# Transposing a feed-forward activation tile with one DMA instead of identity products and PSUM copies

## What is computed

```python
def _bitlinear(x, w, b):
    xn = _layer_norm(x)
    xq = _activation_quant(xn)      # round(x * 127 / max|x|), clipped, / scale
    wq = _weight_quant(w)           # -1, 0, 1 times a scale
    return jnp.einsum('bsd,fd->bsf', xq, wq) + b
h = _bitlinear(x, w1, b1)           # 512 -> 2048
h = jax.nn.gelu(h, approximate=False)
return _bitlinear(h, w2, b2)        # 2048 -> 512
```

## Time and profile before

| | |
|---|---|
| median of 3 runs | 1193.89 us |
| lowest and highest run | 1190.55 and 1193.91 us |
| span of the profiled execution | 1187.8 us |
| its own time | no other than the span is shown; the median of the runs is 6.1 us more |
| mean granted TensorE clock | 0.944 |
| TensorE busy in the span | 1066.7 us, 90% |
| VectorE, ScalarE, GpSimd | 894.3 us, 721.0 us, 610.7 us |
| stage of the change | 237 to 405 us |

### The profile page before, as it was taken

How to read it: one execution, slowest core, us unless ns; L and a number is a source line. 1 busy time by engine, 2 the same in 40 slices (tenths; PEclk the granted TensorE clock), 3 DMA queues, 4 the chain that set the end, 5 groups by cost and what they waited for, 6 DMA issues and landing times. The chain is left out here.

```text
span 1187.8 us, 25724 instructions
## 1 busy us (share of the span) xinstructions
PE 1066.7 (90%) x9595; PEld 800.0 (67%) x9691; DVE 894.3 (75%) x1650; ACT 721.0 (61%) x1134; POOL 610.7 (51%) x629
## 2 busy tenths in 40 slices
PE   5999997679999899968999998788999799999995
PEld 4777776635554567727777776488776688888883
DVE  5589998978888798667888888578985556555538
ACT  4565772669899555638888877376454345545430
POOL 4444445635555322337788888421586355555520
PEclk9999998979999999979999999856999899999998
DMA  8573531043334212331222220096597567778877
GB/s 306 185 252 123 165 91 63 1 151 107 106 107 140 108 32 95 93 110 28 55 57 58 58 56 19 2 347 226 153 263 243 178 227 242 245 242 279 310 280 293
DMA packets 75744, 181.10 MB, mean 152 GB/s; under 512 B 9920, under 2 KB 12118, under 8 KB 74700
## 3 DMA queue, kind: packets, MB, share of 16 engines
q1 hardware_dynamic: 59292, 135.90, 34.4%
q0 software_dynamic: 8544, 24.68, 6.6%
q10 hardware_dynamic: 7792, 18.96, 5.2%
HBM read 128.49 MB, written 44.47 MB: 146 GB/s over the span
## 5 line engine op out<-in xcount | busy, mean ns | idle before, releaser
L470 PE MATMUL ps_y<-kv,toep 128*128 128x288 f32 x640 | 157.8, 409 | 3.6 <-PEq L173 2.0
L470 PEld LDWEIGHTS ps_y<-kv,toep 128*128 128x128 f32 x640 | 122.1, 192 | 38.7 <-DMA toep<-taps_padded 2.6
L1662 POOL TENSOR_TENSOR vw<-at_pf,kw 128x1024 bf16<-128x1024 f32 x64 | 136.6, 2134 | 2.7 <-ACT kw L1722 2.7
L164 POOL TENSOR_TENSOR kv<-kx 128x1024 f32<-128x1024 f32 x32 | 60.6, 1894 | 85.4 <-PE ps_y L470 35.8
L2648 POOL DMA_INDIRECT expert_results<-e_yo,target x47 | 70.3, 1496 | 55.3 <-ACT e_yo L2695 55.3
L1718 ACT ACTIVATE at_pf<-ps_st 128x1024 f32<-128x1024 f32 x64 | 65.5, 1024 | 40.7 <-PE ps_st L1858 36.5
L1769 DVE TENSOR_REDUCE at_negmax<-ps_s 128x4 f32<-128x1024 f32 x64 | 78.3, 1224 | 2.8 <-PE ps_s L1819 0.9
L1138 PEld LDWEIGHTS ps_eg<-e_xT,e_w 128*128 128x128 bf16 x1128 | 67.9, 99 | 14.9 <-issue 2.2
L1138 PE MATMUL ps_eg<-e_xT,e_w 128*128 128x128 bf16 x1128 | 71.9, 221 | 3.9 <-DVE e_xT L2756 3.9
L1077 PE MATMUL ps_fH<-w1T,f_qaT 128*128 128x512 bf16 x253 | 64.6, 400 | 9.8 <-PEq L643 5.5
L2749 DVE COPY e_w<-expert_weights 128x4096 bf16 x47 | 57.7, 1227 | 19.6 <-issue 19.6
(11 more groups left out here) (470 smaller groups left out, 3163.0 us busy)
## 6 DMA issues: line engine op xcount, KB each, us to landing
e_parts<-down_parts SPq DMA_DIRECT2D x47, 512.0 KB, 4.5
w_raw<-in_L_ffn_w ACTq DMA_DIRECT2D x32, 512.0 KB, 4.5
toep<-taps_padded SPq DMA_DIRECT2D x32, 256.0 KB, 3.6
f_draw<-in_L_ffn_rw SPq DMA_DIRECT2D x16, 512.0 KB, 4.3
down_parts<-f_dparts SPq DMA_DIRECT2D x16, 512.0 KB, 2.9
expert_weights<-expert_results SPq DMA_DIRECT2D x16, 512.0 KB, 9.9
x_res<-in_x SPq DMA_DIRECT2D x4, 1024.0 KB, 11.1
c_in<-in_ctx SPq DMA_DIRECT2D x4, 1024.0 KB, 14.2
```

The source lines that it names most:

```text
L164: pool.tensor_tensor(pairs[:, :, :, 0:HD0], x[:, :, 0:HD0].unsqueeze(2).broadcast_to([P, ROWS_N, WIDE, HD0]), sliding_rows(x, 0, 1, WIDE), ...
L470: last = pe.matmul(y[:, l * B:(l + 1) * B, :, WIDE - 1:], toep[h % 2][:, (DC - 1 - l + m) * P:(DC - l + m) * P], kv[h % 2][:, m * B:(m + 1 ...
L1662: pool.tensor_tensor(pl[u % 4][:, :, :, :], pf[u % 2][:, :, :, :], ph[u % 4][:, :, :, :], ALU.subtract)\
```

## The change

TensorE's 16 identity products for `f_qb`, the PSUM tiles' copies on ScalarE and VectorE and their semaphore `qbT_psum` are gone. In their place SP issues one `dma_start_transpose` a tile, from `f_qb` in SBUF (128 x 2048 bf16, 512 KB) to `f_qbT` in SBUF (128 x 16 x 128), ahead of the store and the load of the same turn. It waits for the rounding of the tile, and from tile 2 on for the down product of the tile two before it, which read the same `f_qbT` buffer. Its semaphore rises by 16 for a transfer, one semaphore for each buffer. `down(t)` waits once for the whole transfer, and `round_h(t)` from tile 2 on waits until the transfer of tile t-2 has read `f_qb`. The PSUM tiles `ps_fQ` stay, for the bias rows that are turned in the first steps.

```diff
--- before.py
+++ after.py
@@ -792,7 +792,7 @@
         qa_ready, qaT_psum, qaT_ready = quantised.qa_ready, quantised.qaT_psum, quantised.qaT_ready
         h_psum, gelu_done, dequant_kept = sem("hp"), sem("gelu"), sem("dk")
         rstd_ready, centred, quant_ready, h_scaled, qb_ready = (sem(n) for n in ("rstd", "cent", "quant", "hsc", "qb"))
-        qbT_psum, y_psum, y_added, biased = (sem(n) for n in ("qbTp", "yp", "ya", "biased"))
+        y_psum, y_added, biased = (sem(n) for n in ("yp", "ya", "biased"))
         parts_ready, parts_psum, rows_ready = quantised.parts_ready, quantised.parts_psum, quantised.rows_ready
         qbT_ready = [sem("qbT0"), sem("qbT1")]
         d_loaded, d_stored = ([sem(f"{n}{i}") for i in range(2)] for n in ("dl", "ds"))
@@ -807,6 +807,8 @@
         others_var, others_rstd = sem("ov"), sem("ors")
         GROUPS = (FIRST_TILES, OTHER_TILES)
 
+        DMA_INC = 16
+        turns_up_to = lambda t, p: (t - p) * (DMA_INC // 2) + DMA_INC
         runs = lambda j: not known(j) or 0 <= j < NT
         later = lambda j: not known(j) or j >= 2
 
@@ -842,10 +844,17 @@
                         row = ROWS[place] + 2 * e
                         sp.dma_start(rows[row:row + 2, :], k.ins[name][e, :].rearrange("(c p) -> c p", p=P)).then_inc(ahead_loaded, 16)
 
+            def turn_qb(t):
+                sp.wait_ge(qb_ready, t + 1)
+                if t >= 2:
+                    sp.wait_ge(y_psum, t - 1)
+                sp.dma_start_transpose(qbT[t % 2][:, :, :], qb[t % 2][:, :]).then_inc(qbT_ready[t % 2], DMA_INC)
+
             load(0)
             load(1)
             load_ahead()
             for e in range(E_N):
+                turn_qb(e)
                 sp.wait_ge(d_low, e + 1)
                 sp.dma_start(expert_down_parts(k)[e, :, :], d_parts[e % 2][:, :, :].rearrange("p h n -> p (h n)")).then_inc(d_stored[e % 2], 16)
                 if e + 2 < E_N:
@@ -874,10 +883,6 @@
                 scales.normalised(link, dve, OTHER_TILES)
                 scales.quantisers(k, link, dve, OTHER_TILES)
 
-            def copy_qbT(t, p):
-                dve.wait_ge(qbT_psum, t * 2 + 2)
-                dve.tensor_copy(qbT[p][:, 8:, :], psQ[1][:, :, :]).then_inc(qbT_ready[1], 1)
-
             def centre(t, p):
                 dve.wait_ge(gelu_done, t * 2 + 2)
                 link(dve.tensor_scalar(col(p, NEG_MEAN), col(p, SUM), col(p, OTHER_SUM), -1.0 / FF, ALU.add, ALU.mult))
@@ -898,6 +903,8 @@
 
             def round_h(t, p):
                 dve.wait_ge(h_scaled, t + 1)
+                if later(t):
+                    dve.wait_ge(qbT_ready[p], turns_up_to(t, p) - DMA_INC)
                 dve.tensor_scalar(qb[p][:, :], h[p][:, :], ROUND, None, ALU.subtract).then_inc(qb_ready, 1)
 
             def add_y(t, p):
@@ -944,8 +951,6 @@
                     round_h(n, p)
                 if runs(n + 1):
                     farthest(n + 1, 1 - p)
-                if runs(n):
-                    copy_qbT(n, p)
                 if runs(n + 1):
                     scale_of(n + 1, 1 - p)
 
@@ -983,10 +988,6 @@
                 act.wait_ge(squared, t + 1)
                 act.activation(col(p, VAR), col(p, SQUARE_SUM), ACT.Identity, scale=1.0 / FF, bias=k.small[:, 3:4]).then_inc(var_ready, 1)
 
-            def copy_qbT(t, p):
-                act.wait_ge(qbT_psum, t * 2 + 1)
-                act.activation(qbT[p][:, 0:8, :], psQ[0][:, :, :], ACT.Copy).then_inc(qbT_ready[0], 1)
-
             def scale(t, p):
 
                 act.wait_ge(quant_ready, t + 1)
@@ -1085,21 +1084,11 @@
                                          b1_parts[0:BIAS_ROWS, f * 512:(f + 1) * 512], start=False, stop=True)
                     last.then_inc(h_psum, 1)
 
-            def transpose_qb(t, p):
-                pe.wait_ge(qb_ready, t + 1)
-                for g in range(2):
-                    if not known(t) or t:
-                        pe.wait_ge(qbT_ready[g], t)
-                    for c in range(8):
-                        last = pe.transpose(psQ[g][:, c, :], qb[p][:, (8 * g + c) * P:(8 * g + c + 1) * P], k.ident_b[:, :])
-                    last.then_inc(qbT_psum, 1)
-
             def down(t, p):
                 if not known(t) or t:
                     pe.wait_ge(y_added, t)
+                pe.wait_ge(qbT_ready[p], turns_up_to(t, p))
                 for c in range(FC):
-                    if c % 8 == 0:
-                        pe.wait_ge(qbT_ready[c // 8], t + 1)
                     last = pe.matmul(psY[:, :], qbT[p][:, c, :], k.w2T[:, c * D:(c + 1) * D],
                                      start=(c == 0), stop=(c == FC - 1))
                 last.then_inc(y_psum, 1)
@@ -1109,8 +1098,6 @@
                     up(n + 1, 1 - p)
                 if runs(n + 2) and not (known(n) and n == -2):
                     transpose_qa(n + 2, p)
-                if runs(n - 1):
-                    transpose_qb(n - 1, 1 - p)
                 if runs(n - 2):
                     down(n - 2, p)
 
```

## The result

Kernel after: median of 7 runs 1188.61 us (1186.04 to 1190.20); kernel before, on the same chip: median of 7 runs 1193.79 us. **The ratio is 0.995, with a 95% interval of 0.993 to 0.9971: 5.2 us faster, by the interval 3.5 to 8.4 us.** In a second comparison, after 12 runs against before 35, the ratio is 0.9955 (0.9933 to 0.9976) and the medians are 3.7 us apart.

The account below looks back on a forecast made before the run. The prediction took the 9.04 us cycle of VectorE and GpSimd to bound the loop, not TensorE. Head -2.3 and tail -0.4 us gave 1193.9 - 2.7 = 1191.2 us, range 1186 to 1205.

Parts of the forecast that it names:

- rival D: In the looped tiles TensorE is the bound after all: eleven periods fall by 1.06 us, time 1179; chance 0.08.
- the ring: In the feed-forward loop VectorE and GpSimd wait for each other every tile; this 9.04 us cycle sets the period.
- part 2: PSUM copies removed: VectorE's 16 x 0.68 = 11 us become longer waits; ScalarE's removal counts only at the head and the tail.
- the head: At tile 0 ScalarE is freed of its copy and wait; tile 1's rounding starts 2.3 us earlier, bounds 0 and 2.7.
- the transfer: SP's 512 KB transposing transfer lands 4.6 us after the rounding, between 2.9 and 6.4; it costs the loop nothing.
- rival A: Transfers on one queue set the period: at 16 us each near 1295 us, at 10 us +11 us; chance 0.20.
- the split case: Eight SBUF-to-SBUF transfers of 64 KB, issued within 4.94 us, last landing at 6.4 us: upper estimate for the transfer.
- the tail: Last down product waits for the landing, runs 1.5 us slow, ends 404.4 against 404.51: gain 0.1 us, called 0.4.
- the sum: Gains at the head and the tail together: -2.3 - 0.4 = -2.7 us, bounds -5.0 and -0.6.
- Rival B: Landing in 6.4 to 9 us: the loop holds, the tail pays; at 9 us +2 us, 1196; chance 0.09.
- the last step of the working: Whole kernel: median 6.1 us above the 1187.8 us span, untouched by the change, so 1193.9 - 2.7 = 1191.2 us.
- no difference: Whole kernel's time within about 0.3%, 3.6 us, of before; chance 0.50, against 0.28 faster and 0.22 slower.

Follow-up runs that it names:

- experiment 1: Kernel after with 16 identity products of a constant put back on TensorE each tile, nobody waiting for them: 1189.68 us, ratio 0.9961 to the kernel before.
- experiment 4: Kernel after with the transposing transfer issued later, behind the store of the expert parts: 1196.49 us, ratio 1.0017 to the kernel before.
- 2: Kernel after with GpSimd's inverse root for the next tile moved ahead of its expert-weight split: 1190.74 us, ratio 0.9962 to the kernel before.
- 3: Kernel before with GpSimd's inverse root for the next tile moved ahead of its expert-weight split: 1196.89 us, ratio 1.0023 to the kernel before.
- 9 to 12: Inverse root between GpSimd's cast and subtraction: kernel after 1176.04 us; after with products back 1179.92; kernel before 1188.77; after with tile 15 by products 1178.40.
- Experiment 8: Kernel before with both PSUM copies on VectorE, TensorE's products kept, no transposing transfer: 1188.98 us, ratio 0.9985 to the kernel before.
- The second execution of after: Kernel after, unchanged, measured and profiled once more: 1186.08 us, ratio 0.9955 to the kernel before, stage 164.32 us.
- the second pair of traces: Both kernels unchanged, profiled once more: before 1192.54 us, stage 168.80 us; after 1186.08 us, stage 164.32 us.

## Why the prediction was right, and where not

**Right, the bound.** "Nothing of TensorE, nor any DMA, is in it": the 9.04 us period stayed to 0.01 us when TensorE's products went, stayed when they came back (experiment 1), stayed when the transfer landed 4.5 us later (experiment 4), and moved only when the order of GpSimd's work did (2, 3 and 9 to 12). TensorE's 82.30 of 84 us was occupancy, not a bound (rival D). Still, it had little to spare: "were the ring shorter by a microsecond, TensorE would be the bound and the removal would count" held, and sooner than that. With the products TensorE needs 8.9 us a tile, so 0.3 us off the 9.2 were enough. Two things were missing from the sentence. Without the products it is VectorE, at 8.65 us, and not TensorE that is full next. And the 0.68 us copy that part 2 wrote off as a longer wait then counts as well: the kernel before is at 8.90 us in the loop, where the kernel after with the products but without the copy stays at 8.65 up to tile 9. That is less than 0.68 in part because the collision is lighter there (L616 1.31 and L617 0.43 us in every other tile).

**Right, the head.** Forecast 2.3 us with tile 1's rounding at 266.06; measured 2.43 us, at 265.60 with a stage that began 0.36 us earlier. Experiment 8 has ScalarE's part of the cause at work without the transfer. The bound of 2.7 us held.

**Right, the transfer.** Forecast 4.6 us, measured 4.3 us median, 4.4 us for the last one; rival A (10 to 16 us each) is out. The nearest rows, one issue of 512 KB, led to it; the split case of eight 64 KB transfers would have led to 6.4. Of the two figures of the Trainium skill, "DMA: Bandwidth & Descriptors" (2.0 us by its 261 GB/s) was low by half as an estimate, and "VectorE: DVE Perf Modes" (an estimate of 21 us, from 1309 ns a block) five times high. The measurement decides: whatever a single block takes, sixteen in one transfer take 4.3 us. The queue was priced less well: I gave SP's issue no length of its own, and it is 1.3 to 2.0 us in place of 0.34 for a plain store, 3.33 when it comes right behind one.

**Right, the mechanism of the tail; its 0.4 us by luck.** The down product was to wait for the landing, not for L915: it did (396.02, L915 ended 395.37), near the 397 that was named, and it ran slowly as priced (5.30 us, forecast 3.63 + 1.5). The working gave 0.1 us and was raised to 0.4 for a part-warm clock. Measured were 2.81 - 2.43 = 0.4: 0.13 us behind the last rounding, and 0.26 us between the roundings of tiles 12 and 15, which the sum did not have. The second execution of after has 1.5 us more behind the last rounding, so this part is no better known than that. What ends the stage there is VectorE's own work behind its two subtractions, which the working did not price. Rival B had the mechanism right and the price nearly: a landing 4.4 us later was to cost 4.3 us, and in experiment 4 one 6.3 us later cost 7.8, 1.15 of them by a down product slower than after's.

**Wrong, the last step of the working:** "6.1 us more, which the change does not touch". The profiled execution after is 1189.1 us for a span of 1187.3, so 1.8 us lie outside the span, not 6.1. By that measure the profiled execution of before (span 1187.8) was about 1189.6 us, below the lowest of its timed runs, 1190.55. It was a quick one, and the sum from its span was right for the stage but was laid on a median that has more in it. It did no harm, since a difference was carried over.

**Open: the rest of the gain.** 5.2 us were measured (3.5 to 8.4), where the stage gives 2.8 in the first pair of traces and 4.5 in the second (168.80 to 164.32), 3.6 on average. What lies outside the stage, span less stage, is 1019.5 and 1024.3 us in the two traces of before, and 1021.8 and 1018.6 in the two of after: it varies by 5 us within a kernel. Most of that lies in the experts' loop: from its first weight copy (L2749 before, L2736 after) to the first L2812 (L2799 after) it is 228.3 and 231.4 us before, 231.3 and 229.5 us after, with no order by kernel. The stage's part is within the interval's reach, and no run here settles whether 1 to 2 us more come from elsewhere. The forecast of 1191.2 us was 2.6 us above the median, inside its range; "no difference" had the largest chance at 0.50 because the sum was below 3.6 us, and the result lies just beyond that line. The measured 5.2 us also lie just beyond the sum's own bound of 5.0. The mechanism was right; what fell short is the size of the whole, and of it the traces show only the end of the stage, worth 1.5 us more in the second execution.

## What to carry to other kernels

A busy share near 100% does not make an engine the bound: follow who waits for whom round one period, and test with the same load added back. Before pulling work out of such a ring, look at what the wait it causes had kept apart; the better place for the root was between two GpSimd instructions, not ahead of both. And a change that relieves an engine beside the path is worth measuring again once the path is shortened: here its value went from 2.8 us (4.5 in the second pair of traces) to 11.8 us of a 165 us stage.

## What was not expected of the hardware

- VectorE and GpSimd slow each other in both directions. L616 goes from 0.55 to 1.2 or 1.6 us and L617 from 0.43 to 1.38 us beside GpSimd's L1034 or L1021; GpSimd's cast goes from 1.04 to 1.96 us and its subtraction from 2.13 to 2.98 us beside VectorE's L920 and L924, and L924 itself from 1.21 (L917 at the end of the kernel before) to 2.06 and 2.48 us. The 2.28 us maximum L893 beside the same cast and subtraction is unchanged, and so are they; so is the 0.68 us copy out of PSUM (L879) beside the subtraction in the kernel before with the root between.
- One transposing transfer of 512 KB from SBUF to SBUF lands in 4.3 us, and SP is busy 1.3 to 2.0 us issuing it. In the loop it raises the mean DMA share from 0.36 to 0.65, yet the f_draw loads land in 4.3 us and the stores in 2.9 us, as in the earlier trace rows.
- The 16 down products of the last tile take 3.61 us after TensorE has stood idle 2.43 us, 5.30 after 3.34 us and 6.45 after 6.11 us, at mean granted clocks of 1.00, 0.68 and 0.55 while they run. The length of the idling alone does not decide it: before tile 13's down product TensorE idles 4.30 us in both executions of after, and the product takes 5.21 us (clock 0.69) in one and 6.51 us (clock 0.55) in the other. In the loop the clock is 1.00.
